# Products of zeros on TensorE in its two early waits

## The reference

```
xn = layernorm(x)
s = tanh(beta * (spin + global + softmax attention over spin))    # spin = xn W_spin + b
g = silu(sigmoid(xr W_r) * (relu(xk W_k)^2 W_v))                  # xr, xk: token mixes
x = x + s * g
xn = layernorm(x)
s = (retention over 16 heads with decay masks, normed) * (xn W_g + b_g), times W_o
g = silu(soft mixture of 8 experts, 64 slots each: dispatch, gelu MLP, combine)
x = x + s * g
```

## Time and profile before

| | before |
|---|---|
| median of 3 runs | 1070.06 us (1069.85 to 1070.55) |
| the profiled execution | 1069.8 us, span of its instructions 1068.0 us |
| TensorE busy | 1040.6 us, 97% of the span |
| VectorE, ScalarE, GpSimd busy | 918.3, 810.7, 414.8 us |
| mean granted clock of TensorE | 0.996 |

### The profile page before, as it was taken

How to read it: one execution, slowest core, us unless ns; L and a number is a source line. 1 busy time by engine, 2 the same in 40 slices (tenths; PEclk the granted TensorE clock), 3 DMA queues, 4 the chain that set the end, 5 groups by cost and what they waited for, 6 DMA issues and landing times.

```text
span 1068.0 us, 27273 instructions
## 1 busy us (share of the span) xinstructions
PE 1040.6 (97%) x10244; PEld 822.9 (77%) x10244; DVE 918.3 (86%) x1818; ACT 810.7 (76%) x1434; POOL 414.8 (39%) x555
## 2 busy tenths in 40 slices
PE   5799999999999999999999999999999999999997
PEld 3478787787878778787887878878787787877866
DVE  3788898888988888988889988889998888988785
ACT  4486877778787886877778787887877878777775
POOL 2433535324343333534325343343533335343240
PEclk9899999999999999999999999999999999999999
DMA  6000000000000000000000000000000000000000
GB/s 262 12 2 11 2 21 2 22 1 2 21 2 21 2 12 11 2 22 1 22 2 2 21 2 21 2 11 12 2 21 2 13 10 1 22 1 12 2 12 10
DMA packets 18463, 16.85 MB, mean 16 GB/s; under 512 B 800, under 2 KB 17440, under 8 KB 18080
## 3 DMA queue, kind: packets, MB, share of 16 engines
q1 hardware_dynamic: 18336, 15.12, 4.4%
HBM read 10.93 MB, written 4.19 MB: 14 GB/s over the span
## 4 chain that ended last, share of the span: by engine, by line
PE 94%; DVE 2%; issue 1%; ACT 1%; POOL 0%; DVEq 0%; ACTq 0%; POOLq 0%
PE bank L1023 13%; PE bank L979 11%; PE bank L969 11%; PE bank_s L1000 7%; PE bank L989 6%; PE bank L960 5%; PE bank L930 5%; PE bank L825 3%; PE bank L856 3%; PE bank L923 3%; PE bank L910 3%; PE bank L952 3%; PE bank_s L1003 3%; PE bank L876 3%; PE bank L1030 3%; PE bank L1038 2%
## 5 line engine op out<-in xcount | busy, mean ns | idle before, releaser
L326 POOL TENSOR_TENSOR ret_abs<-ret_abs 128x512 f32<-128x512 f32 x128 | 181.4, 1421 | 250.5 <-ACT ret_abs L479 250.3
L659 DVE TENSOR_TENSOR ret<-bank_s,k_sb 128x1536 f32<-128x1536 f32 x128 | 223.7, 1748 | 29.5 <-PE bank_s L1003 19.9
L479 ACT ACTIVATE ret_abs<-ret 128x1536 f32<-128x1536 f32 x128 | 189.7, 1482 | 26.8 <-DVE ret L659 26.8
L979 PEld LDWEIGHTS bank<-w_sb,hact 128*128 128x128 f32 x1024 | 127.9, 191 | 18.0 <-issue 7.8
L979 PE MATMUL bank<-w_sb,hact 128*128 128x128 f32 x1024 | 138.6, 278 | 0.0
L333 POOL TENSOR_SCALAR dT<-dT,drec 128x256 f32<-128x256 f32 x128 | 67.2, 542 | 170.2 <-DVE drec L723 170.2
L969 PE MATMUL bank<-slotsT,w_sb 128*128 128x128 f32 x1024 | 130.1, 275 | 0.4 <-ACT slotsT L469 0.4
L969 PEld LDWEIGHTS bank<-slotsT,w_sb 128*128 128x128 f32 x1024 | 123.2, 192 | 1.7 <-ACT slotsT L469 0.8
L474 ACT ACTIVATE hact<-hact 128x512 f32<-128x512 f32 x128 | 80.1, 627 | 52.1 <-DVE hact L728 51.8
L1023 PE MATMUL bank<-ret,vrow 128*32 128x256 f32 (+1 forms) x2048 | 108.2, 329 | 0.3 <-POOL ret_abs L326 0.3
L1000 PE MATMUL bank_s<-qT,km 32*128 32x256 f32 x1024 | 91.4, 426 | 0.9 <-POOL km L320 0.6
(11 more groups left out here) (143 smaller groups left out, 2266.4 us busy)
## 6 DMA issues: line engine op xcount, KB each, us to landing
x_sb<-x SPq DMA_DIRECT2D x16, 256.0 KB, 2.9
w_sb<-w SPq DMA_DIRECT2D x2, 2048.0 KB, 13.8
out<-attn SPq DMA_DIRECT2D x16, 256.0 KB, 2.3
v_sb<-vectors SPq DMA_DIRECT2D x1, 705.0 KB, 7.2
k_sb<-consts SPq DMA_DIRECT2D x1, 538.0 KB, 5.9
w_sb<-weights SPq DMA_DIRECT2D x1, 512.0 KB, 4.4
w_sb<-weights SPq DMA_DIRECT2D x1, 320.0 KB, 3.4
slot_sb<-slot_rows SPq DMA_DIRECT2D x1, 256.0 KB, 3.6
```

The source lines that it names most:

```text
L326: pool.tensor_tensor(both[:, :, P:SEQ], both[:, :, P:SEQ], both[:, :, SEQ:3 * P], ALU.add)\
L479: act.activation(ret_abs[:, q % MR], ret[:, q % MR], ACT.Abs).then_inc(ready["ab"].sem, 1)
L659: dve.tensor_tensor(ret[:, q % MR], bank_s[:, :, 0:3 * P], causal.unsqueeze(1).broadcast_to([P, Q, 3 * P]), ALU.mult)\
L979: ins = pe.matmul(bank[:, i * C:(i + 1) * C], hact[:, i, c], w2_sb[:, e, c], start=(c == 0), stop=(c == HC - 1))
```

## The change

A helper on TensorE, `turn_over(times)`, multiplies the first 512 columns of `vrow` by its first 128, all zeros at that time, and writes the 128x512 product into the fourth bank of `bank_s`. It is called with 3 at the head of TensorE's stream, behind a wait for GpSimd's four clears and ahead of the wait for `early`, and with 8 behind the four transposes of `slots_across`.

```diff
         @block.tensor
         def _(pe):
 
+            def turn_over(times):
+
+                for _ in range(times):
+                    pe.matmul(bank_s[:, 3], still[:, 0:P], still, start=True, stop=True)
+
+            still = vrow[:].rearrange("p j h v -> p (j h v)")[:, 0:512]
+            pe.wait_ge(ready["setup"].sem, 4)
+            turn_over(3)
             pe.wait_ge(early.sem, 48)
...
                 for j in range(4):
                     ins = pe.transpose(bank_s[:, 0, j * P:(j + 1) * P], slot_sb[:, j], ident)
                 ins.then_inc(filled["setup"].sem, 1)
+                turn_over(8)
```

## The result

| | before | after |
|---|---|---|
| median | 1070.16 us (6 runs, 1069.73 to 1070.55) | 1065.42 us (6 runs, 1065.09 to 1067.08) |
| profiled execution, its span | 1069.8, 1068.0 us | 1065.09, 1063.3 us |
| mean granted clock | 0.996 | 0.999 |

The ratio is 0.996, 95% interval 0.9947 to 0.9973: 4.7 us faster, where 1065.5 us was forecast. The six runs are not one cluster: four took 1065.1 to 1065.4 us, two took 1066.8 and 1067.1 us at a mean clock of 0.997 and 0.998.

What follows compares the result with a forecast made beforehand. TensorE bounds the kernel, without slack from 60 us on, so only its idle and half-clock work before that counts. 3.1 us at the head plus 1.4 us behind the slots make 4.5 us: median 1065.5 us, range 1064.5 to 1066.8 us.

Steps and rivals of the forecast that it cites:

- the gain of the first 60 us goes through whole: TensorE from 60 us on has no slack, so reaching that stretch X us earlier ends the program X us earlier.
- The first half: Three products at the head: clock up for xn's transposes, s and e; L381 earlier by 3.1 us (2.5 to 3.5).
- ScalarE without a hole from L387 to L381: ScalarE after its copy of e: no more wait for gbias, so L381 at 15.31 us against 18.40 us.
- The loads: Slot and v_sb transfers that ScalarE's squares need: last landed at 11.8 us, 1.3 us to spare.
- Reading the clock: First hole on TensorE: go by durations, worth about 3 us; by the granted clock the first half would be worth nothing.
- the clock stays up in the thin stretch: TensorE from 8 to 20 us: the clock holds over the new sequence's longest hole, 1.7 us.
- rival 1: First loads hold ScalarE, or clock falls in the thin stretch; only the second half pays: 1068.1 to 1068.7 us; chance 0.08.
- The second half: Eight products behind the slots' transposes: clock stays up before xn2T, kT earlier by 1.4 us (1.0 to 1.9).
- rival 2: Both blocks: zeros do not raise or hold the clock; 1070.1 to 1070.7 us; chance 0.06.
- Slower by a clock that is down under the eight: Eight products run wholly at the lower clock, products after xn3T start 5.3 us later: 1075 us; chance 0.04.
- Eaten later, between 43 and 60 us: VectorE or ScalarE later than TensorE in the second round, up to 1.4 us lost: 1066.5 to 1067.5 us; chance 0.06.

Runs made afterwards that it cites:

- e1: Changed kernel without the eight products behind the slots, only the three at the head: 1067.44 us, ratio 0.9975 to the kernel before.
- e2: Changed kernel without the three products at the head, only the eight (new wait kept): 1068.47 us, ratio 0.9983 to the kernel before.
- e9: Changed kernel with one product of zeros at the head, not three; the eight stay: 1068.35 us, ratio 0.9982 to the kernel before.
- e8: Changed kernel with sixteen products of zeros behind the slots, not eight: 1071.22 us, ratio 1.0011 to the kernel before.
- e3: Changed kernel with the same eleven products streaming two columns each, not 512: 1070.36 us, ratio 1.0000 to the kernel before.
- e10: Changed kernel with four products behind the slots, not eight; the three stay: 1067.44 us, ratio 0.9974 to the kernel before.

## Why the prediction was right

**What bounds.** That the gain of the first 60 us goes through whole held: 4.59 us of lead at 55 us, 4.7 us at the end, TensorE busy 959.63 of 960 us in both.

**The first half.** Forecast 3.1 us (2.5 to 3.5); 3.16 us at L381 in the trace. e1's 2.8 us by the median is less because its second low stretch was longer, not because the first half gave less: its xn2T starts 3.26 us earlier. The terms: transposes 1.09 to 0.63, s and e 2.04 to 1.10 (I had 1.02, the length of one that follows other work without a hole), ScalarE without a hole from L387 to L381 as worked out, 15.24 us for 15.31. The loads were no hindrance.

**Reading the clock.** Going by durations and not by the granted clock of the earlier trace rows for the first 17 us was the decisive choice. e2 and e9 show products of 2.05 us under a record of 1.00, at mean clocks of 0.999 to 1.000.

**That the clock stays up in the thin stretch** is the step that held only in most runs. I argued from holes (1.2 us, and 5.0 us of none at all) that 1.7 us could do no harm. e8 shows it fall at 11.8 us, not in the longest hole but in one of 1.20 us, with another of 0.84 us before it and less than 2 us of work since the rise. Why it fell there is open. That rival 1 named (the clock goes down again in the thin stretch), but at 1068.1 us or more; a long run is only 1.1 to 1.8 us longer, and in the one traced the clock is up again after 3.4 us, under the work that follows. The median was spared since about three runs in four are not long: on this step the forecast was lucky.

**The second half.** Forecast 1.4 us (1.0 to 1.9); 1.4 us between the traces of before and after, 1.7 us by e2's median, 2.1 us between the traces of e1 and after. The forecast took its size from the one trace of before, in which the low stretch lasted 6.8 us; in e1 and e3 it lasted 10.2 us. The block was forecast at 6.86 us of issue with 0.4 us of slack, and it had 0.28 us; e8 and e10 show one point on either side: eight more cost nearly their whole length, four fewer gained nothing.

**The rivals.** Zeros do hold the clock: granted 1.00 from 22.7 to 34 us under them. The Trainium skill ("TensorE: Matmul & The Clock Gate", Part 1) had said that activity releases the throttle; the traces agree for products of zeros too, with s and e at 1.10 us behind three of them. In the sum of rival 2 there is a slip: up to the fall at 31.08 us 6.0 of the eight would have fitted ((31.08 - 25.92) / 0.86), not 5.8, which moves its end by 0.2 us and decides nothing. Slower by a clock that is down under the eight: not seen in any of the traces; e8's sixteen took 0.43 us per record even in a long run. Eaten later, between 43 and 60 us: no, the lead is 4.58 us at kT and 4.59 us at L864.

## What to carry to other kernels

Judge a filler by the first work behind the hole: it pays if the clock is up there. Here a hole of 0.28 us left behind the filler was harmless and one of 3.7 us cost the whole gain (e10); nothing between the two was tried. A filler twice too long cost 5.9 us (e8). Compare durations of like instructions, not only the granted clock, to see whether a start is cold. And where one warms the clock ahead of a thin stretch, try short fillers inside that stretch: with them none of 20 runs was a long one.

## What was not expected of the hardware

- The granted clock read 1.00 from the span's start up to the first fall in every trace, while in the trace of before 128x512 float32 products took 2.04 us at 9.8 us and 1.02 us at 49 us.
- Products of zeros raise and hold the clock: at the head, three of them (4.37 us in the trace of the changed kernel) were enough, one (2.08 us, then 2.95 us idle) was not, and three of two columns were not.
- From the last work to the fall it was 5.0 us before the change and 3.7 us in e1; in e10 the fall came 3.9 us after the last product of zeros, with xn2T just begun; in e8 it came with no hole longer than 1.20 us. Once down, the clock stayed so for 6.8 us before the change, 10.2 us in e1 and e3, 6.9 us in e10, 3.4 us in e8. What sets these lengths is open.
